# Window attention of 32 images: units of one image by 68 queries, or of two images by 64 queries with the last four apart

## The reference, cut to what matters

```python
q = (x @ Wq + bq).reshape(B, S, H, hd).transpose(0, 2, 1, 3)
k = (x @ Wk + bk).reshape(B, S, H, hd).transpose(0, 2, 1, 3)
v = (x @ Wv + bv).reshape(B, S, H, hd).transpose(0, 2, 1, 3)
scores = jnp.einsum('bhqd,bhkd->bhqk', q, k) * scale
allowed = (j <= i) & (i - j < WINDOW)
scores = jnp.where(allowed, scores, NEG_INF)
attn = jax.nn.softmax(scores, axis=-1)
out = jnp.einsum('bhqk,bhkd->bhqd', attn, v)
return out.transpose(0, 2, 1, 3).reshape(B, S, D) @ Wo + bo
```

## Time and profile before

| what | us |
| --- | --- |
| median of 3 runs (1057.57 to 1058.37) | 1058.24 |
| the execution that was profiled | 1058.27 |
| its span | 1056.5 |
| TensorE busy in the span | 950.1 |
| VectorE busy | 589.3 |
| GpSimd busy | 522.1 |
| ScalarE busy | 412.9 |
| first scores of the attention to the first matmul behind it | 54.95 to 224.45 |

### The profile page before, as it was taken

The page is one execution under the profiler, slowest core; times in us unless marked ns, Lnnn a source line. Parts: engine busy times, 40 slices in busy tenths (PEclk is TensorE's granted clock), DMA queues, the critical chain, the costliest instruction groups (busy, mean ns, idle before and its releaser), DMA issues. The chain is left out here.

```text
span 1056.5 us, 29782 instructions
## 1 busy us (share of the span) xinstructions
PE 950.1 (90%) x10440; PEld 746.9 (71%) x10440; DVE 589.3 (56%) x1463; ACT 412.9 (39%) x1102; POOL 522.1 (49%) x714
## 2 busy tenths in 40 slices
PE   8899999988747999999999999889979947999996
PEld 6667777777634888888888876445546635888895
DVE  1878888865994777433333325678877552111111
ACT  2266776634253344444444422223323222433331
POOL 0056655610604777776777627777773002433332
PEclk9999999999979999999999999989889987999998
DMA  7010000002004988877788723334482046486750
GB/s 257 1 46 2 0 0 0 2 11 75 1 1 165 307 275 254 277 243 224 242 264 255 228 88 100 101 115 120 121 288 82 22 182 228 143 271 215 266 155 26
DMA packets 79821, 149.30 MB, mean 141 GB/s; under 512 B 18892, under 2 KB 53327, under 8 KB 75760
## 3 DMA queue, kind: packets, MB, share of 16 engines
q1 hardware_dynamic: 34768, 77.15, 21.5%
q0 software_dynamic: 17712, 47.88, 15.8%
q10 hardware_dynamic: 27248, 23.09, 6.5%
HBM read 200.22 MB, written 31.73 MB: 220 GB/s over the span
## 5 line engine op out<-in xcount | busy, mean ns | idle before, releaser
L1332 POOL DMA_INDIRECT x_x<-m_x_rows,x_idx x170 | 166.1, 977 | 74.3 <-issue 35.8
L1358 PE MATMUL x_pup<-x_xt,x_w 128*128 128x128 f32 (+1 forms) x2176 | 182.9, 250 | 0.0
L1358 PEld LDWEIGHTS x_pup<-x_xt,x_w 128*128 128x128 f32 (+1 forms) x2176 | 166.9, 165 | 5.9 <-issue 5.7
L1624 POOL DMA_INDIRECT rl_y<-m_y_rows,rl_idx x136 | 134.8, 991 | 43.6 <-issue 37.8
L1439 DVE TENSOR_TENSOR x_hid<-x_gate,x_pup 128x128 f32<-128x128 f32 x170 | 48.9, 288 | 148.2 <-ACT x_gate L1411 142.4
L1372 PE MATMUL x_pdown<-x_w,x_hid 128*128 128x256 f32 (+1 forms) x408 | 104.2, 389 | 0.2 <-DVE x_y L1446 0.2
L1407 ACT ACTIVATE x_xt<-x_pturn 128x256 f32<-128x256 f32 x170 | 65.3, 384 | 89.1 <-PE x_pturn L1343 86.3
L442 POOL TENSOR_TENSOR wa_probs<-wa_probs,wa_peak 68x544 f32<-68x544 f32 x64 | 70.0, 1094 | 57.5 <-DVE wa_peak L593 54.7
L2437 DVE TENSOR_TENSOR x_y<-x_pdown,x_b 128x256 f32<-128x256 f32 x21 | 8.9, 425 | 150.7 <-PE x_pdown L2391 150.7
L2423 ACT ACTIVATE x_hid<-x_pup,x_b 128x128 f32<-128x128 f32 (+1 forms) x200 | 52.8, 357 | 93.7 <-PE x_pup L2374 93.5
L1411 ACT ACTIVATE x_gate<-x_pup 128x128 f32<-128x128 f32 x170 | 47.2, 278 | 92.4 <-PE x_pup L1358 92.4
(11 more groups left out here) (344 smaller groups left out, 1914.8 us busy)
## 6 DMA issues: line engine op xcount, KB each, us to landing
x_w<-in_experts SPq DMA_DIRECT2D x204, 384.0 KB
late_w<-in_w SPq DMA_DIRECT2D x28, 1024.0 KB, 13.3
m_y_rows<-x_y ACTq DMA_DIRECT2D x170, 128.0 KB
xT<-in_w SPq DMA_DIRECT2D x12, 1024.0 KB, 6.1
xn<-in_w SPq DMA_DIRECT2D x10, 1024.0 KB, 10.3
h<-in_w SPq DMA_DIRECT2D x10, 1024.0 KB, 14.0
m_x_rows<-xn SPq DMA_DIRECT2D x34, 128.0 KB, 1.8
x_x<-m_x_rows,x_idx POOLq DMA_INDIRECT x170
```

What stands on the lines that cost most here:

```text
L1332: nc.gpsimd.indirect_dma_start(x[:, s, :], None, x_rows, bass.IndirectOffsetOnAxis(ap=idx[:, s:s + 1], axis=0))\
L1358: mm = nc.tensor.matmul(pup[rows:rows + wide, bank, m * P + side * wide:m * P + (side + 1) * wide], w[:, lane, first:first + wide], xt[:, ...
L1624: nc.gpsimd.indirect_dma_start(y[:, t % YR, kk, :], None, y_rows, bass.IndirectOffsetOnAxis(ap=idx[:, n:n + 1], axis=0))\
```

## The change

A unit is now two images by 64 queries by 8 heads, 128 rows and 512 columns, and there are 32. The mask needs only the first 64 keys there. All loops are written out. The queries 64 to 67 of a **pair** of images, for both column halves, are one small unit of 128 rows (head, query, image) by 68 keys. So a pair is two steps: an even one, in which the scores of its first half and of its last queries are made, and an odd one.

The last queries are spread over heads on GpSimd (`last_spread`, into `lq`), scored by four matmuls behind the main ones of the even step (into columns of the first score bank that the main scores leave free), masked and reduced on VectorE, exponentiated on ScalarE with its own sum, and then multiplied on GpSimd by the reciprocal sum and by tables of zeros and ones (`last_normalise`: 10, 16 and 128 elements wide). TensorE transposes the two results (`last_turn`), weights the values (`last_weigh`), VectorE picks each row's head (`last_pick`), and a last matmul sums rows into queries (`last_sum`).

The sums of the softmax come from VectorE (`add_up`, `invert`) instead of from matmuls against ones, and GpSimd multiplies the probabilities by the reciprocal (`normalise`) before they are transposed. Transposes take two heads at once: four of 128 by 128 a unit instead of eight of 68 by 68. Keys are spread two units ahead of their scores, each in two operations (one an image). A block has seven jobs in four steps, two in each step but the last: the values of two images at once (`v0`, `v1`: eight matmuls in two halves of the output rows), the values of the last tokens (`vt`), and keys and queries of the block ahead. `qT`, `kT` and `vals` have two slots, and the copy `xb` is gone.

```diff
-        "mask": np.where((k <= q) & (q - k < WINDOW), 0.0, NEG),
+        "mask": np.where((k2 <= q2) & (q2 - k2 < WINDOW), 0.0, NEG),
+        "last_mask": np.where((k <= HALF + row_query) & (HALF + row_query - k < WINDOW), 0.0, NEG),
...
-        probs = sb("probs", [S, 4, HC, S])
...
+        probs = sb("probs", [P, 4, HC, HALF])
...
+        pl_score = pscore[:, 0, P:P + S]
...
+            jobs = [[(blk, "v0"), (blk + 1, "q0")], [(blk, "v1"), (blk + 1, "q1")],
+                    [(blk, "vt"), (blk + 1, "k0")], [(blk + 1, "k1")]][n]
...
+                def spread(unit):
+                    c = unit % DC
+                    pool.wait_ge(jobs_moved, done_by(unit, f"k{c}"))
+                    if unit >= 2:
+                        pool.wait_ge(scored, unit - 1)
+                    keys = pair_cols(unit, slice(0, HALF))(kT[:, unit // ABLK % 2, c, :])
+                    for i in range(2):
+                        ins = nc.gpsimd.tensor_tensor(
+                            kheads[:, unit % 2, i, :, :], keys[:, i, :].unsqueeze(1).broadcast_to([P, PER, HALF]),
+                            const("head_of").unsqueeze(2).broadcast_to([P, PER, HALF]), ALU.mult)
+                    ins.then_inc(keys_spread, 1)
...
-                    nc.gpsimd.tensor_tensor(probs[:, slot4, :, :], probs[:, slot4, :, :],
-                                            peak[:, slot2, :].unsqueeze(2).broadcast_to([S, HC, S]),
+                    nc.gpsimd.tensor_tensor(probs[:, unit % 4, :, :], probs[:, unit % 4, :, :],
+                                            peak[:, unit % 2, :].unsqueeze(2).broadcast_to([P, HC, HALF]),
                                             ALU.subtract).then_inc(shifted, 1)
 
-                def body(blk, table):
-                    for step in range(UNITS):
-                        c, b = step // ABLK, step % ABLK
-
-                        if c == 0:
-                            if isinstance(blk, int) and blk == 0:
-                                pool.wait_ge(jobs_moved, 1)
-                            else:
-                                pool.wait_ge(jobs_moved, job_count(blk, 0))
-                        else:
-                            pool.wait_ge(jobs_moved, job_count(blk, JOBS.index(("k1", 1)) + 1))
-                        if not (isinstance(blk, int) and blk == 0 and step < 2):
-                            pool.wait_ge(scored, blk * UNITS + step - 1)
-                        nc.gpsimd.tensor_tensor(
-                            kheads[:, step % 2, :, :],
-                            kT[:, c, b * S:(b + 1) * S].unsqueeze(1).broadcast_to([P, PER, S]),
-                            head_of, ALU.mult).then_inc(keys_spread, 1)
-                        if not (isinstance(blk, int) and blk == 0 and step == 0):
-                            shift(blk * UNITS + step - 1, (step - 1) % 4, (step - 1) % 2)
-                        if step == 6 and table is not last_jobs:
-                            pool.wait_ge(jobs_done, job_count(blk, JOBS.index(("v", 3)) + 1))
-                            nc.gpsimd.tensor_copy(xb[:, :, :], xT[:, :, bass.ds((blk + 1) * CB, CB)])\
-                                .then_inc(block_copied, 1)
-
-                blocks(pool, body)
-                shift(NBLK * UNITS - 1, 3, 1)
+                def normalise(unit):
+                    pool.wait_ge(inverted, unit + 1)
+                    nc.gpsimd.tensor_tensor(probs[:, unit % 4, :, :], probs[:, unit % 4, :, :],
+                                            inv[:, unit % 2, :].unsqueeze(2).broadcast_to([P, HC, HALF]),
+                                            ALU.mult).then_inc(normalised, 1)
...
+                def last_spread(pair):
+                    unit = 2 * pair
+                    pool.wait_ge(jobs_moved, done_by(unit, "q1"))
+                    if pair >= 2:
+                        pool.wait_ge(scored, 2 * (pair - 2) + 1)
+                    for c in range(DC):
+                        queries = pair_cols(unit, slice(HALF, S))(qT[:, unit // ABLK % 2, c, :])
+                        ins = nc.gpsimd.tensor_tensor(
+                            lq[:, pair % 2, c, :, :, :], queries.unsqueeze(2).broadcast_to([P, 2, HC, LAST]),
+                            const("head8").unsqueeze(1).unsqueeze(3).broadcast_to([P, 2, HC, LAST]), ALU.mult)
+                    ins.then_inc(l_spread, 1)
+
+                def last_normalise(pair):
+                    pool.wait_ge(l_inverted, pair + 1)
+                    if pair:
+                        pool.wait_ge(l_turned, pair)
...
+                    pool.wait_ge(l_rows, pair + 1)
+                    nc.gpsimd.tensor_tensor(ltail[:, :, :], lprob[:, pair % 2, HALF:S].unsqueeze(1).broadcast_to([P, ABLK, LAST]),
+                                            lrows[:, pair % 2 * 4:pair % 2 * 4 + 4].unsqueeze(2)
+                                            .broadcast_to([P, ABLK, LAST]), ALU.mult)
+                    nc.gpsimd.tensor_tensor(lmain[:, :, :], lprob[:, pair % 2, 0:HALF].unsqueeze(1).broadcast_to([P, 2, HALF]),
+                                            lrows[:, 8:10].unsqueeze(2).broadcast_to([P, 2, HALF]),
+                                            ALU.mult).then_inc(l_ready, 1)
+
+                spread(0)
+                spread(1)
+                last_spread(0)
+                for step in range(STEPS + 1):
+                    even = step % 2 == 0
+                    if step < STEPS:
+                        shift(step)
+                    if step >= 1:
+                        normalise(step - 1)
+                    if even and 2 <= step <= STEPS:
+                        last_normalise(step // 2 - 1)
+                    if not even and (step + 1) // 2 < NPAIR:
+                        last_spread((step + 1) // 2)
+                    if step + 2 < STEPS:
+                        spread(step + 2)
...
+                def score(unit):
+                    c, slot = unit % DC, unit // ABLK % 2
+                    pe.wait_ge(keys_spread, unit + 1)
+                    pe.wait_ge(jobs_moved, done_by(unit, f"q{c}"))
+                    if unit:
+                        pe.wait_ge(masked, unit)
+                        pe.wait_ge(l_masked, (unit + 1) // 2)
...
+                    if c == 0:
+                        pair = unit // 2
+                        pe.wait_ge(l_spread, pair + 1)
+                        pe.wait_ge(jobs_moved, done_by(unit, "k1"))
...
+                def turn(unit):
+                    pe.wait_ge(normalised, unit + 1)
+                    if unit:
+                        pe.wait_ge(turn_moved, unit)
+                    for two in range(HC // 2):
+                        mm = nc.tensor.transpose(pturn[:, two * P:(two + 1) * P],
+                                                 probs[:, unit % 4, 2 * two:2 * two + 2, :].rearrange("p h n -> p (h n)"), ident)
...
+                def last_turn(pair):
+                    pe.wait_ge(l_ready, pair + 1)
+                    if pair:
+                        pe.wait_ge(l_placed, pair)
+                    nc.tensor.transpose(pl_main, lmain[:, :, :].rearrange("p o n -> p (o n)"), ident)
+                    nc.tensor.transpose(pl_tail, ltail[:, :, :].rearrange("p n q -> p (n q)"), ident).then_inc(l_turned, 1)
...
+                for step in range(STEPS + 3):
+                    jobs = jobs_of(step)
+                    if step < STEPS:
+                        score(step)
+                    if step >= 3:
+                        weigh(step - 3)
+                    if step >= 3 and step % 2 == 1:
+                        last_weigh((step - 3) // 2)
+                    for job in jobs[:1]:
+                        do_job(*job)
+                    if step >= STEPS:
+                        keep_running(3)
+                    if 0 <= step - 2 < STEPS:
+                        turn(step - 2)
+                    for job in jobs[1:]:
+                        do_job(*job)
+                    if 2 <= step < STEPS + 2 and step % 2 == 0:
+                        last_turn(step // 2 - 1)
+                    if step >= 3 and step % 2 == 1:
+                        last_sum((step - 3) // 2)
+                keep_running(3)
...
+                def add_up(unit):
+                    dve.wait_ge(exped, unit + 1)
+                    if unit:
+                        dve.wait_ge(inverted, unit)
+                    nc.vector.tensor_reduce(total[:, :], probs[:, unit % 4, :, :], AX.X, ALU.add).then_inc(summed, 1)
...
+                for step in range(STEPS + 3):
+                    even = step % 2 == 0
+                    if step < STEPS:
+                        mask(step)
+                        if even:
+                            last_mask(step // 2)
+                        find_peak(step)
+                        if even:
+                            last_peak(step // 2)
+                    if 1 <= step <= STEPS:
+                        add_up(step - 1)
```

(41 more changed lines are left out.)

434 lines of the change are left out of this document (221 added, 213 removed).

## The result

The changed kernel takes **1106.26 us** (median of three runs, 1102.86 to 1106.63) against 1058.24: a ratio of 1.0437 with the 95% interval [1.0404, 1.0471]. The execution taken apart took 1106.63 us, with a span of 1104.8. The forecast was 1066.4 with a range up to 1081: the sign was right, the size was not. It lay 40 us too low.

The account below looks back on a forecast made before the run. TensorE bounded the attention; a chain through every engine would replace it, with pairs of 10.26 or 10.67 us against 10.13. The next stage would start 8.2 us later: 1058.3 + 8.2 = 1066.4 us, 8-in-10 range 1054 to 1081.

Parts of the forecast that it names:

- What bounds, and what takes its place: Attention: TensorE bounds before; after, a chain through every engine, with TensorE waiting some 2.5 us in each pair.
- The wait ahead of the last scores: Attention, even step: TensorE's last scores wait for GpSimd's spreading of the last queries, priced 0.60 us in the odd step.
- GpSimd's prices: Attention products on GpSimd: 1.03 us for 512 wide, 0.42 for 128 wide, 0.20 and 0.21 for 10 and 16 wide.
- The rival of dearer products: Attention: wide GpSimd products cost 1.26 us instead of 1.03, 15 us more, 1081 in all; chance 0.17.
- The even step: Attention, from the end of one unit's scores to that of the next, through all engines: 5.67 us.
- The start: Start of the attention: first scores end at 57.1 against 55.4; the first pair's even step takes 8.0 us.
- The drain: End of the attention: 15.4 us after the last scores end at 216.9, where the kernel before needs 9.5.
- the bare chain: Attention: a pair's even and odd steps together take 10.26 us, or 10.67 with two jobs, against 10.13 before.
- The last weighting: Attention, TensorE: eight matmuls of 128 columns for the last queries take 1.07 us, between 0.55 and 1.7.
- The two-job odd step: Attention: in 6 of the pairs the odd step holds two jobs with one PSUM bank and takes 5.00 us.
- The clock: Attention, rival: TensorE's clock falls to the lower of its two levels throughout, 85 us more, 1150; chance 0.04.
- the two rivals above the forecast: Attention: dearer GpSimd products, 1081, chance 0.17; low TensorE clock throughout, 1150, chance 0.04.

Follow-up runs that it names:

- x3: Changed kernel with filler matmuls in TensorE's gap before the last queries' transposes and the last weighting's four main parts ahead of its four tails: 1063.6 us.
- x1: Changed kernel with two or four matmuls whose results nobody reads in TensorE's gap before the last queries' transposes: 1084.56 us.
- x8: Changed kernel with each 16-row matmul of the last weighting replaced by its 128-row neighbour, same output rows and order: 1063.86 us, one execution.
- x10: Changed kernel with the last queries' transposes and following work one step later, their spreading ahead of GpSimd's shift, last weighting still alternating: 1068.26 us.
- x11: Changed kernel with the last weighting's large matmuls first and the last queries' three products on VectorE instead of GpSimd: 1057.85 us.

## Why the prediction was wrong in size

Two steps failed: the price of the last weighting, and the clock, which had no term. All steps, one after another:

- **What bounds, and what takes its place.** Right as far as it went. TensorE waits for GpSimd's last product ahead of its transposes, 18.8 us in 12 waits, as foretold. The wait ahead of the last scores shows only once the last weighting is short: in x3 four times from 100 to 195 us, 0.83 each.
- **GpSimd's prices.** Right: 1.042 us for the 512-wide products (1.03), 0.398 for `lmain` (0.42), 0.213 and 0.205 for the small ones. The rival of dearer products falls. So does the Trainium skill's proportion (GPSIMD Engine Reference, Performance versus the Vector engine), 1.12 us: the rows of this kernel were nearer. The page's figure is for an addition, not a product; here the subtraction (L463) and the product (L469) both took 1.042.
- **The even step** 5.57 (5.67). **The start**: first scores' end at 57.38 (57.1); but the first pair takes 9.9, not 8.0. **The drain**: in x3 213.13 to 228.58, 15.45 us (15.7 with the 0.3 ahead of the next stage). That is close partly by luck: the last weighting is shorter there than was put in, and the clock averages 0.88 from 200 to 228 us.
- **The pair.** In x3 9.86 and 10.11, where the bare chain was put at 10.26 and 10.67; 0.39 of the second difference is the last weighting, 0.68 there instead of 1.07. x3 ends its attention 4.0 before the forecast 232.6.
- **The last weighting: wrong.** "Two in a row go to the same 32 rows, so between 0.55 (all beside) and 1.7 (none), and I take 5 x 0.21 = 1.07." It measured 2.65 in the changed kernel, above the upper bound. The bound assumed that matmuls one after another cost 0.21 each, which is the pace of matmuls of one shape; the property that counted was the number of rows of weights, 128 and 16 in turn, and no row of before had such a change in a tight sequence. The two-job odd step, 5.00 by TensorE's path, so becomes 6.6. Price: **19.5 us** at the full clock (x1 to x3, from 2.65 down to 0.68).
- **The clock: wrong.** The forecast reasoned from "the gaps expected here are shorter" than those of the earlier trace rows, gave the low clock throughout 0.04, and had no term for a low clock in part. It fell for parts of the time, behind gaps of 1.1 to 2.7 us. Price: **20.45 us** (changed kernel to x1), and most of it only because the last weighting had made TensorE the pace there: with the grouping it is 3.0.
- **"Nothing behind it changes":** the code doesn't; 4.2 us came, cause open.

The sum: 20.45 + 19.5 - 4.0 + 4.2 = 40.2 us, which is 1106.6 - 1066.4. The two large terms depend on which loss is taken away first: with the grouping first they are 37.0 and 3.0, and their sum is the same.

The range ended at 1081 because the two rivals above the forecast stood alone: one term over its bound moved the kernel to where the other, held for unlikely, could bite.

## What to carry to other kernels

Put a bound on a group of small matmuls only from rows that mix their shapes as the new code does; otherwise count a full matmul, start to end (0.33 us here), for each change of the weights' row count, and write equal shapes next to each other, which cost nothing here. When a new wait appears on TensorE, price the clock with it: gaps of one to three microseconds in each round were enough here, in some kernels and not in others, so read the granted clock, and it is dearest where TensorE's own work is nearly the pace. And before work is given up as slower, ask whether the wait belongs to the idea or to the place in the order: the same units with the last weighting grouped and the last queries' transposes one step later take 1044.69 us, with their spreading earlier too 1041.39, and with two jobs exchanged 1031.0, all faster than both kernels.

## What the runs showed of the hardware

- Matmuls of 128 and of 16 rows of weights in turn, on 32 output rows each, start 0.33 us apart at the full clock and 0.56 at the low one (changed kernel); grouped, a group of four takes 0.34 (x3); all of one height, eight take 0.58 (x8).
- The granted clock fell to 0.50 in or behind some of the gaps of 1.1 to 2.7 us on TensorE that came once in 10 to 12 us. It stayed at 1.00 when two or four matmuls that compute nothing stood in them (x1, 100 to 228 us), or when the order left no such gap (x10, 100 to 200 us), but also with gaps of 0.59 and 1.13 us (x11, 70 to 200 us).
- A VectorE product of two operands in SBUF, 16 elements a row, took 0.91 us beside a wide GpSimd product (x11); VectorE's 512-wide reductions, with one operand, kept their 0.68 in the same run.
